# Routing weights picked in the first stage, and the dispatch of a mixture of experts copies them

## The reference

```python
qkv = xn @ Wqkv                                   # 512 -> 3 x 512
k, v = conv(k), conv(v)                           # grouped, 4 tokens -> 1, 16 heads
attn = softmax(mask(q @ [null_k, k].T * d ** -0.5)) @ [null_v, v]
branch1 = real(fft(fft(attn @ W_out + b_out, axis=-1), axis=-2))

scores = sigmoid(xn @ router_w.T)                 # 64 experts in 8 groups
topk_idx = top 8 experts by scores + e_bias, within the 4 best groups
w = scores[topk_idx] / sum(scores[topk_idx])
branch2 = shared_mlp(xn) + sum over the 8 of w * expert_mlp(xn)
```

## Time and profile before

| | us |
|---|---|
| median of 3 runs (5633.38 to 5650.49) | 5639.76 |
| the profiled execution, its own time | 5632.38 |
| span of the profiled execution | 5630.6 |
| PE busy | 5462.3 |
| DVE busy | 3849.7 |
| POOL busy | 2996.2 |
| ACT busy | 2578.8 |
| first instruction of the second stage | 778.82 |

### The profile page before, as it was taken

The page is one execution under the profiler, slowest core; times in us unless marked ns, Lnnn a source line. Parts: engine busy times, 40 slices in busy tenths (PEclk is TensorE's granted clock), DMA queues, the critical chain, the costliest instruction groups (busy, mean ns, idle before and its releaser), DMA issues. The chain is left out here.

```text
span 5630.6 us, 101187 instructions
## 1 busy us (share of the span) xinstructions
PE 5462.3 (97%) x33072; PEld 4555.4 (81%) x33072; DVE 3849.7 (68%) x7136; ACT 2578.8 (46%) x3737; POOL 2996.2 (53%) x2620
## 2 busy tenths in 40 slices
PE   8999979999999999999899999999999999999999
PEld 7888866666666666776899999999999999999886
DVE  5444438887778877776666666666666666666656
ACT  3222223333333333333566666666666666666510
POOL 2222202555555555411677777777777777777514
PEclk9999989999999999999999999999999999999999
DMA  6555454434444344432667667677788667676648
GB/s 222 179 179 179 172 161 121 120 110 135 117 129 128 111 130 122 128 113 90 142 116 155 127 130 178 133 156 156 166 206 195 134 118 171 134 155 112 153 173 286
DMA packets 478101, 836.09 MB, mean 148 GB/s; under 512 B 54273, under 2 KB 159490, under 8 KB 475251
## 3 DMA queue, kind: packets, MB, share of 16 engines
q1 hardware_dynamic: 337011, 541.90, 30.3%
q0 software_dynamic: 140928, 292.13, 28.9%
HBM read 501.55 MB, written 332.30 MB: 148 GB/s over the span
## 5 line engine op out<-in xcount | busy, mean ns | idle before, releaser
L1649 POOL DMA_INDIRECT mid_base<-e_rows,e_ox x556 | 1179.0, 2120 | 371.1 <-POOL e_ox L1644 255.7
L1758 DVE TENSOR_TENSOR e_wgu_lo<-e_wgu,e_wgu_hi 128x2048 fp32r<-128x2048 f32 x278 | 637.3, 2292 | 812.5 <-ACT e_wgu_hi L1681 728.8
L1637 POOL DMA_INDIRECT e_xg<-mid_xn,e_ix x556 | 623.2, 1121 | 338.8 <-POOL e_ix L1634 228.0
L1694 ACT CAST e_xT_hi<-e_ps_t 128x512 fp32r<-128x512 f32 x556 | 298.9, 590 | 951.8 <-PE e_ps_t L1824 951.8
L935 POOL DMA_INDIRECT mid_ids<-b_pairs,b_cell x512 | 608.7, 1189 | 148.9 <-issue 147.5
L1837 PE MATMUL e_ps_g<-e_xT_hi,e_wgu_hi 128*128 128x256 f32 x2224 | 652.6, 293 | 1.7 <-DVE e_gated L1775 1.7
L1837 PE MATMUL e_ps_g<-e_xT_lo,e_wgu_hi 128*128 128x256 f32 x2224 | 629.6, 283 | 0.0
L1837 PE MATMUL e_ps_g<-e_xT_hi,e_wgu_lo 128*128 128x256 f32 x2224 | 629.5, 283 | 0.0
L1837 PE MATMUL e_ps_u<-e_xT_hi,e_wgu_lo 128*128 128x256 f32 x2224 | 629.4, 283 | 0.0
L1837 PE MATMUL e_ps_u<-e_xT_hi,e_wgu_hi 128*128 128x256 f32 x2224 | 629.4, 283 | 0.0
L1837 PE MATMUL e_ps_u<-e_xT_lo,e_wgu_hi 128*128 128x256 f32 x2224 | 629.4, 283 | 0.0
(11 more groups left out here) (257 smaller groups left out, 13413.2 us busy)
## 6 DMA issues: line engine op xcount, KB each, us to landing
b_q<-mid_q_hi SPq DMA_DIRECT2D x128, 256.0 KB
b_xT_hi<-mid_xT_hi SPq DMA_DIRECT2D x32, 1024.0 KB
b_xT_lo<-mid_xT_lo SPq DMA_DIRECT2D x32, 1024.0 KB
mid_base<-b_x SPq DMA_DIRECT2D x32, 1024.0 KB, 7.0
e_wgu<-in_gate_w SPq DMA_DIRECT2D x62, 512.0 KB
e_wgu<-in_up_w SPq DMA_DIRECT2D x62, 512.0 KB
e_wd<-in_down_w SPq DMA_DIRECT2D x62, 512.0 KB
ec_cell<-mid_base SPq DMA_DIRECT2D x88, 256.0 KB, 5.1
```

What stands on the lines that cost most here:

```text
L1637: pool.indirect_dma_start(xg[s][:, i, :], None, t["xn"], bass.IndirectOffsetOnAxis(ap=ix[s][:, i:i + 1], axis=0))\
L1649: pool.indirect_dma_start(t[f"base{i}"], bass.IndirectOffsetOnAxis(ap=ox[s][:, i:i + 1], axis=0), rows[s][:, i, :], None, compute_op=ALU.a ...
L1694: act.copy(xT_hi[s][:, i * DC // 2 * RB:(i + 1) * DC // 2 * RB], ps_t[i][:, :]).then_inc(xT_hi_ready, 1)
L1758: dve.tensor_tensor(wgu_lo[s][:, :], wgu[s][:, :], wgu_hi[s][:, :].bitcast(F32), ALU.subtract)\
```

## The change

- `stage_a` loads a row of the numbers 1 to 64 (NLOADS 10), and DVE runs a new function, `pick`, between `route` and `split_x`: sel times number, MAX8 (the eight experts in falling order), and for each rank k an is_equal, a multiply by w and a reduce into `w8[:, :, k]`. SP stores w8 (8 per token, 16 KB a step) and no longer w.
- The wait ahead of the convolution of k is for eight copies of the projection; one for all twelve stands ahead of the convolution of v.
- `stage_b` loads w8 whole (256 KB) before q of the second unit, and the table on DVE waits for it too. `load_group` loads pos only. `group` keeps instructions 0 to 10, gets one copy of the eight weights per token in place of the 24, and has 13 instructions; they go to every third slot of the same three units, the last one to the last slot.

```diff
@@ stage_a, SP
                 hold(sp, emptied["pos"], nth("pos", s, 0), passed)
                 sp.dma_start(t["pos"][:, bass.ds(s * TPB * EXPERTS, TPB * EXPERTS)],
-                             posm[:, :, :].rearrange("p a e -> p (a e)")).then_inc(wp_out, 16)
-                sp.dma_start(t["w"][:, bass.ds(s * TPB * EXPERTS, TPB * EXPERTS)],
-                             w[:, :, :].rearrange("p a e -> p (a e)")).then_inc(wp_out, 16)
+                             posm[:, :, :].rearrange("p a e -> p (a e)")).then_inc(pos_out, 16)
+                hold(sp, w8_ready, s + 1, passed)
+                sp.dma_start(t["w8"][:, bass.ds(s * TPB * TOPK, TPB * TOPK)], w8[:, :, :].rearrange("p a k -> p (a k)"))\
+                    .then_inc(w8_out, 16)
@@ stage_a, DVE
+            def pick(s, st, first):
+
+                key, eq = taken, (masked, ptmp)
+                st.mark(dve.tensor_tensor(key[:, :, :], sel[:, :, :], number[:, None, :].broadcast_to([P, TPB, EXPERTS]),
+                                          ALU.mult))
+                st.hold()
+                for i in range(TPB):
+                    st.mark(dve.max(best[:, i, :], key[:, i, :]))
+                st.wait()
+                if first:
+                    dve.wait_ge(route_ready, 1)
+                else:
+                    dve.wait_ge(route_ready, s + 1)
+                    dve.wait_ge(w8_out, 16 * s)
+                for k in range(0, TOPK, 2):
+                    for i in range(2):
+                        st.mark(dve.tensor_tensor(eq[i][:, :, :], key[:, :, :],
+                                                  best[:, :, k + i:k + i + 1].broadcast_to([P, TPB, EXPERTS]), ALU.is_equal))
+                    st.wait()
+                    for i in range(2):
+                        st.mark(dve.tensor_tensor(eq[i][:, :, :], eq[i][:, :, :], w[:, :, :], ALU.mult))
+                    st.wait()
+                    for i in range(2):
+                        st.mark(dve.tensor_reduce(w8[:, :, k + i], eq[i][:, :, :], AX, ALU.add))
+                    st.hold()
+                dve.sem_inc(w8_ready, 1)
...
                 route(s, st, first)
+                pick(s, st, first)
                 if not last:
                     split_x(s + 1)
@@ stage_a, PE
                 b = bank_free("kc", 0, s, first)
-                pe.wait_ge(emptied["qkv"], nth("qkv", s, 11))
+                pe.wait_ge(emptied["qkv"], nth("qkv", s, 7))
...
                 b = bank_free("vc", 0, s, first)
+                pe.wait_ge(emptied["qkv"], nth("qkv", s, 11))
@@ stage_b, SP
-                for dst, src in ((pos, t["pos"]), (w, t["w"])):
-                    sp.dma_start(dst[r][:, :, :].rearrange("p a e -> p (a e)"), src[:, cols]).then_inc(group_in[r], 16)
+                sp.dma_start(pos[r][:, :, :].rearrange("p a e -> p (a e)"), t["pos"][:, cols]).then_inc(group_in[r], 16)
...
             sp.dma_start(bidx[:, :], t["bidx"]).then_inc(tab_in, 16)
+            sp.dma_start(w8[:, :], t["w8"]).then_inc(tab_in, 16)
             load_q(1)
@@ stage_b, DVE
-                elif e < 35:
-                    k, stage = (e - 11) // 6 * 2 + (e - 11) % 2, (e - 11) % 6 // 2
...
+                elif e == 11:
+                    mark(dve.tensor_copy(pairs[r][:, :, 1].bitcast(F32), w8[:, g * 4 * TOPK:(g + 1) * 4 * TOPK]))
...
-            dve.wait_ge(tab_in, 32)
+            dve.wait_ge(tab_in, 48)
...
-                    if 0 <= g < NG:
-                        group(g, part * SLOTS + k)
+                    at = part * SLOTS + k
+                    if 0 <= g < NG and (at % 3 == 0 or at == GU_UNITS * SLOTS - 1):
+                        group(g, -(-at // 3))
```

More of the change, by code:

```diff
@@ L186, in stage_a @@
         vc_out = sem("a_vc_out")
-        wp_out = sem("a_wp_out")
+        pos_out = sem("a_pos_out")
+        w8_ready = sem("a_w8_ready")
+        w8_out = sem("a_w8_out")
         spare_zeroed = sem("a_spare_zeroed")
@@ L271, in _ @@
             sp.dma_start(t["cnt"], carry[:, :]).then_inc(cnt_out, 16)
-            for s_, n in ((xn_out, 1), (xT_out, 2), (q_out, 2), (kc_out, 2), (vc_out, 1), (wp_out, 2)):
+            for s_, n in ((xn_out, 1), (xT_out, 2), (q_out, 2), (kc_out, 2), (vc_out, 1), (pos_out, 1), (w8_out, 1)):
                 sp.wait_ge(s_, 16 * n * NSTEP)
@@ L606 @@
 GU_UNITS = 3
-GOPS = 36
+GOPS = 13
 def stage_b(nc, t):
@@ L650, in stage_b @@
         pos = [sb(f"pos{r}", [P, 4, EXPERTS]) for r in range(2)]
-        w = [sb(f"w{r}", [P, 4, EXPERTS]) for r in range(2)]
+        w8 = sb("w8", [P, NTILE * TOPK])
         slot = sb("slot", [P, 4, EXPERTS])
-        tmp = [sb(f"tmp{r}", [P, 4, EXPERTS]) for r in range(2)]
         s8 = sb("s8", [P, 4, TOPK])
@@ L666, in stage_b @@
         bidx = sb("bidx", [P, 3])
-        bcmp = tmp[0][:, 0:3, :]
+        bcmp = slot[:, 0:3, :]
         bexp = sb("bexp", [P, 3])
@@ L2213, in internal @@
         kc_hi=d("kc_hi", (DC, P, TOK // CF)), kc_lo=d("kc_lo", (DC, P, TOK // CF)), vc=d("vc", (TOK // CF, DIM)),
[L2214 removed]
+        xT_hi=d("xT_hi", (DC, P, TOK)), xT_lo=d("xT_lo", (DC, P, TOK)), base0=d("base0", (TOK + P, DIM)), base1=d("base1", (TOK + P, DIM)), w8=d("w8", (P, NTILE * TOPK)), pos=d("pos", (P, NTILE * EXPERTS)),
         cnt=d("cnt", (P, EXPERTS)), ids=d("ids", (NSLOT, 2), I32), blk=d("blk", (1, 3 * P), I32), used=d("used", (1, 3), I32),
@@ L2266, in layout @@
         b_out_col=np.ascontiguousarray(a(L0_attn_b_out).reshape(DC, P).T),
-        router_t=np.ascontiguousarray(a(L0_ffn_router_w).T), e_bias_row=rows(L0_ffn_e_bias),
+        router_t=np.ascontiguousarray(a(L0_ffn_router_w).T), e_bias_row=rows(L0_ffn_e_bias), e_number_row=rows(np.arange(1, EXPERTS + 1)),
         gate_w=a(L0_ffn_gate_w), up_w=a(L0_ffn_up_w), down_w=a(L0_ffn_down_w),
```

13 lines of the change are left out of this document (7 added, 6 removed).

## The result

The changed kernel takes 5592.9 us (median of 4 runs, 5589.7 to 5601.3) against 5639.4 (4 runs): ratio 0.9918, 95% interval 0.9899 to 0.9936, so 46.5 us or 0.8% faster. The forecast was 5574, its range 5536 to 5598. The direction and the range held, the range by 5 us; 65 us were expected and 46.5 came.

What follows compares the result with a forecast made beforehand. PE, busy 5462.3 of 5630.6 us, was taken as the bound. Gains of 13.4 (waits) and 53 (dispatch) less 0.5 and 0.8 (loads) made 65 us, from 5639.8 to 5574; range 5536 to 5598.

Steps and rivals of the forecast that it cites:

- Parted waits: First stage: the convolution of k starts 0.84 us earlier in each of 16 steps, gaining 13.4 us, at least 10.9.
- The pick: First stage: 11.4 us more DVE work per step, hidden in 15.64 us of idle time before xT_lo, costing nothing.
- the pick reaches the path: Slower rival, first stage: a pick beyond 23.9 us a step delays PE; at 31 us it gives 5689 us; chance 0.03.
- Loads: The number table at the start costs 0.5 us; loading w8 ahead of q in the second stage costs 0.8.
- Dispatch: Second stage: lighter DVE dispatch gives back 4.7 us per item (3.7 to 5.9), 53 us in all.
- own experiment: Second stage: an item takes 117.75 us with dispatch and scatters, 111.87 with scatters alone, 109.19 with neither.
- I assume that the 2.68 us stay: Second stage: the 2.68 us per item that come with the scatters remain, because the scatters are not touched.
- The convolution doesn't start earlier: Rival, first stage: a bank or another copy holds the convolution; gain 52 us, 5588 us; chance 0.05.
- POOL takes over: Rival, second stage: POOL's scatters and masks limit shorter units, half the dispatch gain goes; gain 39 us, 5601; chance 0.13.
- Everything comes back: Rival, second stage: the scatters' excess goes with dispatch too; gain 89 to 102 us, middle 5545 us; chance 0.22.
- The signs: Expected profile: no L567 wait for ACT, DVE idle near 4 us, second stage near 766, items near 113, last twelve units unchanged.
- Items over 115 us: Second stage: items staying above 115 us, where near 113 was expected, would show the forecast wrong.

Runs made afterwards that it cites:

- Experiment 4: Changed kernel with the pick's loop over the eight ranks run twice (5583.7 us) or three times (5725.6 us, one run).
- sitting 3: Third session of timed runs: kernel before 5632.4 us, changed kernel 5593.2, changed kernel with each unit's scatters in two bunches 5537.5.
- experiment 1: Two kernels: the changed one with the two waits joined again, 5614.2 us; the one before with only the waits parted, 5619.4 us.
- two bunches: Changed kernel with five of a unit's scatters moved ahead of POOL's product with the reciprocals, five or six left behind it: 5537.5 us, earlier 5538.1.
- sitting 2: Second session of timed runs: kernel before 5599.8 us, changed kernel with scatters split in two 5538.1, with the pick's ranks twice 5583.7, three times 5725.6.

## Why the prediction was right, and where it was off

*Parted waits: right.* 13.4 us were forecast. From the first projection matmul to the second stage it took 753.5 us before (25.35 to 778.82) and 739.8 after (28.50 to 768.32), a gain of 13.7, though the first projection matmuls of the profiled run of after were slow (0.63 us where they took 0.40). The window with the waits joined is 15.2 us longer, and the step is shorter by 0.96 us, 15.4 in 16 steps: the 0.84 of the gap, and 0.11 by which the convolution itself is shorter (3.73 us, 3.84 before). Alone, the edit gave 16.3 us of the whole. The wait in the list (10.9) was too small, and the gap between matmuls (0.84 x 16) the better guide, as argued.

*The pick: its cost right, its cover mis-told.* 11.4 us were forecast, 11.0 measured; idle time before xT_lo 4.2 forecast, 4.71 measured. The stage lost nothing. But the rival "the pick reaches the path" added 15.64 us of idle time and 8.2 of slack and put the point at 23.9. Slack is used once: a step that is 8 us late stays 8 us late, and the next one has none. Only idle time comes again in every step, here 15.64 and the 3.51 before L512, 19.2 in all. Experiment 4 shows it: a chain of pick of 20.8 us already costs, where the prediction had it free.

*Loads: small, as said, and not resolved.* PE's wait for q grew by 0.67 us, 0.8 forecast, but it varies by as much between profiles of one kernel (5.3 and 5.8 before, 5.9 and 6.4 after). The table of numbers has no visible cost: the first projection starts at 24.95 us in the changed kernel of sitting 3, and at 25.65 in the one before.

*Dispatch: the step that failed.* "DVE's dispatch costs 5.88 us per item, and scatters a further 2.68" was read from one stretch of four units, 111.87 us. It isn't typical: the same four units take 113.9 to 114.1 in the changed kernel twice and in both kernels of experiment 1, and 112.7 in the other profile of before. So scatters alone cost 3.5 to 4.9 us an item in these, and the trace's "own experiment" gave the difference to dispatch. Alone, dispatch costs 4.56 and what stays of it 0.97 (1.2 forecast); their difference, 3.6, lies at the lower end that the prediction kept. (It wrote 3.7; 5.88 less twice 1.2 is 3.5.) With scatters beside it only 2.2 to 2.6 come through, because part of the delay is hidden by the scatters' own: 5.0 of the 6.0 that an item is still over 109.2 are theirs. "I assume that the 2.68 us stay" was the weak sentence, right that they stay and wrong in their size. This is 53 - 27.4 = 26 us, more than the whole shortfall, which is 22 us by the spans and 18.5 by the medians; what lies between is the parted wait's surplus and the run-to-run part named above. That the range held is in part luck: 39.3 us, the gain of sitting 3, taken from the 5639.8 would be 5600, just outside.

*What else moved.* 3.2 us were lost at the start of the profiled run: the router product took 7.09 us where it took 3.79. It isn't the change's: in sitting 3 the projection of the same kernel began at 24.95, and in experiment 1 that of the kernel before with its waits parted began at 28.76.

*The rivals.* "The convolution doesn't start earlier" (5588) came nearest in time and is refuted: it starts 0.84 us earlier. "POOL takes over" (5601) was next, and its reason isn't the one either. Its sign was that POOL is no longer idle before its masks, and it still is, 90.2 us in the 44 units (85.6 before); what the scatters delay are events to DVE and ACT, not POOL's own work. "Everything comes back" (5545) didn't come with this change, but the time is there: two bunches reach 5537.5 in sitting 3. As the prediction used it, the rule of the Trainium skill ("GPSIMD Engine Reference", Key points), that VectorE and POOL contend for SBUF interfaces when VectorE's instruction has two SBUF inputs or runs in a 2-port mode, would have had such instructions shorter without scatters beside them. For scatters the rows don't show this (L1158, two SBUF inputs: 808 and 797 ns). For POOL's own long pass they agree: the cast of sel beside it took 4.61 us as before, and the pass with two inputs of experiment 4 took 4.73.

*The signs.* No wait of L600 for ACT, DVE's idle time near 4 us, a stage start of 768.3 (766 named) and the last twelve units unchanged all hold. "Items over 115 us" was the sign for being wrong, and they are at 115.2.

## What to carry over

Before a price is read from one stretch of a trace that lacks an ingredient, look whether it repeats (the same four units took 111.9, 112.7 and 113.9 us in three profiles of the same second stage), and take out each of two costs that overlap in time by itself, since their sum isn't the price of either. When work is moved under cover, count the engine's idle time per period; slack behind it can be spent only once. Where scatters go out in long runs, split them, but look first what SP has queued behind the instruction that they would delay.

## What the hardware showed that I had not expected

- Ten or eleven indirect scatters in a row (0.96 us each and 0.30 between them) come with late semaphore events of other engines: DVE's wait for the same matmul is 5.6 us in place of 2.8, under the label "remote". With bunches of five and six neither of DVE's two waits shows it. In the two profiles of the changed kernel the 21 late waits of b_hT ended with the tenth or eleventh scatter of a run already issued, the 23 on time after eight or nine. The mechanism isn't shown.
- The kernel before takes 5632 to 5639 us in two sittings (and in the first comparison) and 5600 to 5603 in two others, and in sitting 2 kernels with one long bunch had no "remote" wait at b_hT at all. Whether this is the whole of the 36 us, and what sets it, stays open. The changed kernel itself wasn't timed in such a sitting. An estimate of what the change brings there is 58 us: the kernel with the pick twice took 5583.7 in sitting 2, less the 42 of its longer first stage 5542, against 5599.8.
- The router product at the start took 3.79 or 7.09 us with nothing different ahead of it; windows there show a granted clock of 1.00 in both.
- Short waits of PE come with longer matmuls: 24 us of waits with 18 us in the first stage with the pick twice, 25.6 us of idle time with 31.0 in the 44 units of one bunch against two. Where PE sets the pace, as in the latter, both are lost; where DVE does, as in the former, the slower matmuls only take the place of waits.

The fastest version found is the changed kernel with two bunches, 5537.5 us: 1.0% below the changed kernel in the same sitting and 1.7% below the one before.
